# Attention block on one Trainium2 core: the inverse row sums reach the other partitions by VectorE's 32x32 turns and an HBM scratch instead of TensorE transposes

## The reference

```python
def _qkv_attention(qkv):
    bs, length, width = qkv.shape
    ch = width // (3 * N_HEADS)
    q, k, v = jnp.split(qkv, 3, axis=-1)
    scale = 1.0 / np.sqrt(np.sqrt(ch))
    q = (q * scale).reshape(bs * N_HEADS, length, ch)
    k = (k * scale).reshape(bs * N_HEADS, length, ch)
    v = v.reshape(bs * N_HEADS, length, ch)
    weight = jnp.einsum('btc,bsc->bts', q, k)
    weight = jax.nn.softmax(weight.astype(jnp.float32), axis=-1).astype(qkv.dtype)
    a = jnp.einsum('bts,bsc->btc', weight, v)
    return a.reshape(bs, length, -1)

xf = x.reshape(b, -1, c)                      # b = 16, 1024 tokens, c = 512
h = _group_norm(xf, norm_scale, norm_bias)    # 32 groups
qkv = h @ qkv_w + qkv_b
h = _qkv_attention(qkv)                       # 8 heads of 64
h = h @ proj_w + proj_b
return (xf + h).reshape(b, *spatial, c)
```

## Time and profile before

| | us |
|---|---|
| median of 3 runs | 3426.82 (3425.06 to 3427.06) |
| the profiled execution | 3426.32 |
| its span | 3424.6 |
| PE busy in it | 3355.7 (98%) |
| DVE busy | 2813.5 (82%) |
| ACT busy | 2085.2 (61%) |
| POOL busy | 1645.7 (48%) |

### The profile page before, as it was taken

One profiled execution on the slowest core, in us unless ns is written; L12 is line 12 of the kernel. 1 busy time (PEld: TensorE's weight loads), 2 busy tenths in 40 slices (PEclk: granted clock), 3 DMA queues, 4 the chain that ended last, 5 costly groups with the idle time before them and its releaser, 6 DMA issues.

```text
span 3424.6 us, 67790 instructions
## 1 busy us (share of the span) xinstructions
PE 3355.7 (98%) x24640; PEld 2542.3 (74%) x24640; DVE 2813.5 (82%) x3473; ACT 2085.2 (61%) x3985; POOL 1645.7 (48%) x2762
## 2 busy tenths in 40 slices
PE   5999999999999999999999999999999999999998
PEld 4777777777777777777777777777777777777775
DVE  4888888888888888888888888888888888888886
ACT  4666665665665656656666566666566666665663
POOL 3444454545545444544444445445454544454552
PEclk9999999999999999999999999999999999999999
DMA  3878778777887877878788787877878778787777
GB/s 114 194 182 196 193 189 197 183 197 189 192 194 185 197 189 192 197 185 195 187 196 194 186 197 182 198 191 190 196 184 198 191 189 198 182 196 189 185 188 177
DMA packets 255707, 646.87 MB, mean 189 GB/s; under 512 B 73872, under 2 KB 73872, under 8 KB 255376
## 3 DMA queue, kind: packets, MB, share of 16 engines
q1 hardware_dynamic: 235792, 604.79, 74.6%
q10 hardware_dynamic: 19584, 37.76, 3.1%
HBM read 71.84 MB, written 33.55 MB: 31 GB/s over the span
## 4 chain that ended last, share of the span: by engine, by line
PE 88%; DVE 4%; ACT 4%; issue 1%; SPq 1%; POOL 1%; DMA 0%; DVEq 0%; POOLq 0%; ACTq 0%
PE pv_ps L373 23%; PE s_ps L344 22%; PE c_ps L407 7%; PE c_ps L408 7%; PE c_ps L409 7%; PE c_ps L419 3%; PE c_ps L421 3%; PE c_ps L420 3%; PE c_ps L391 3%; PE c_ps L393 3%; PE c_ps L392 3%; PE pv_ps L355 3%; DVE turned L610 2%; ACT staged L495 2%; ACT probs L475 2%; PE s_ps L440 2%
## 5 line engine op out<-in xcount | busy, mean ns | idle before, releaser
L475 ACT ACTIVATE probs<-s_ps,neg_max 128x1024 f32<-128x1024 f32 x1024 | 1140.9, 1115 | 821.6 <-DVE neg_max L627 818.4
L627 DVE TENSOR_REDUCE neg_max<-s_ps 128x1 f32<-128x1024 f32 x1024 | 1205.3, 1219 | 411.4 <-PE s_ps L344 411.4
L610 DVE STREAM_TRANSPOSE turned<-probs 128x1024 f32<-128x1024 f32 x1024 | 1233.6, 1229 | 89.9 <-ACT probs L475 70.4
L373 PE MATMUL pv_ps<-probs_t,v 128*64 128x256 f32 x8192 | 943.7, 383 | 6.7 <-DMA probs_t<-turned 6.7
L373 PEld LDWEIGHTS pv_ps<-probs_t,v 128*64 128x64 f32 x8192 | 567.4, 137 | 358.4 <-issue 99.7
L407 PE MATMUL c_ps<-h_hi,w_hi 128*128 128x256 f32 x2048 | 602.7, 294 | 16.7 <-ACT staged L490 8.9
L408 PE MATMUL c_ps<-h_lo,w_hi 128*128 128x256 f32 x2048 | 580.1, 283 | 0.0
L409 PE MATMUL c_ps<-h_hi,w_lo 128*128 128x256 f32 x2048 | 579.5, 283 | 0.0
L495 ACT ACTIVATE staged<-c_ps,qk_bias 64x256 f32<-64x256 f32 x1024 | 481.0, 470 | 125.8 <-PE c_ps L409 112.4
L783 POOL COPY inv_wide<-inv_sum 128x256 f32<-128x256 f32 x256 | 101.5, 397 | 817.4 <-PE pv_ps L355 810.0
L407 PEld LDWEIGHTS c_ps<-h_hi,w_hi 128*128 128x128 f32 x2048 | 392.8, 192 | 20.7 <-ACT staged L490 10.7
(11 more groups left out here) (71 smaller groups left out, 5094.8 us busy)
## 6 DMA issues: line engine op xcount, KB each, us to landing
probs_t<-turned SPq DMA_DIRECT2D x4096, 128.0 KB, 2.4
x_res<-in_x SPq DMA_DIRECT2D x128, 256.0 KB, 3.0
result<-x_res ACTq DMA_DIRECT2D x128, 256.0 KB, 3.1
x_next<-in_x SPq DMA_DIRECT2D x120, 256.0 KB, 3.5
probs_t<-in_L_conv_qkv_w ACTq DMA_DIRECT2D x4, 768.0 KB, 9.0
turned<-in_x SPq DMA_DIRECT2D x4, 512.0 KB, 13.0
probs_t<-in_L_conv_proj_w ACTq DMA_DIRECT2D x4, 256.0 KB, 14.0
v_bias<-in_L_conv_qkv_b SPq DMA_DIRECT2D x1, 256.0 KB, 17.0
```

The lines of the kernel that those rows point to most:

```text
L373: last = nc.tensor.matmul(pv_ps[side][CH * par:CH * (par + 1), 0, :], v_sb[:, ring_of(i, parity), CH * chunk:CH * (chunk + 1)], p_t[:, par ...
L475: nc.scalar.activation(probs[k % 2][:, :], s_ps[k % 2][:, :], ACT.Exp, bias=neg_max[:, k % 4:k % 4 + 1], accum_out=row_sum[:, (k // HALF) ...
L610: nc.vector.transpose(dst, probs[k % 2][:, :].rearrange("p (k b j) -> p k b j", k=CHUNKS, b=QUADS)).then_inc(probs_turned, 1)
L627: nc.vector.tensor_reduce(neg_max[:, k % 4:k % 4 + 1], s_ps[k % 2][:, :], AX.X, ALU.max, negate=True).then_inc(max_ready, 1)
```

## The change

The inverse takes another way. VectorE writes the four reciprocals of a half into the first 4 columns of a 128x32 tile inv_sum, whose other columns GpSimd sets to 1 once at the start. VectorE turns that tile in 32x32 blocks (turn_inverse, at k = 4n+4, behind the scaling): in each quadrant of 32 partitions the first four now hold the inverses of 32 tokens. ScalarE's queue writes these four rows of each quadrant to an HBM scratch, inv_rows, which then holds four rows of 128 (keep_inverse, four transfers of 4x32, at k = 4n+6), and reads them back at k = 4n+10, each pair of rows repeated over 64 partitions, into inv_wide (spread_inverse, two transfers of 64x2x128). VectorE's scaling now waits for that transfer itself, and multiplies pv_ps by inv_wide. The two transposes on TensorE, GpSimd's copy and ScalarE's copy are gone, and pv_ps needs only half its columns. TensorE's wait for the scaling of two halves ago goes from the transposes to attend.

```diff
 MOVE_LAG = 4
-SPREAD_LAG = 8
+KEEP_LAG = 6
+SPREAD_LAG = 10
 ATTEND_LAG = 10
 EVAC_LAG = 12
...
-        inv_sum = sb("inv_sum", [P, 2, HALF])
-        inv_wide = sb("inv_wide", [P, HALF * CH])
+
+        inv_sum = sb("inv_sum", [P, Q])
+        inv_turned = sb("inv_turned", [P, Q])
+        inv_wide = sb("inv_wide", [P, 2, P])
+        inv_rows = nc.dram_tensor("inv_rows", [2, HALF, P], F32, kind="Internal").ap()
...
-        pv_ps = [ps(f"pv_ps{i}", [P, 2, 2 * P]) for i in range(2)]
+        pv_ps = [ps(f"pv_ps{i}", [P, 2 * P]) for i in range(2)]
...
-            def spread_inverse(b, k):
-                n = (k - SPREAD_LAG) // HALF
-                half, side = 2 * BLOCKS * b + n, n % 2
-                pe.wait_ge(inv_widened, half + 1)
-                at_least(pe, attn_scaled, half - 1)
-                for u in range(2):
-                    last = nc.tensor.transpose(pv_ps[side][:, 1, u * P:(u + 1) * P], inv_wide[:, u * P:(u + 1) * P],
-                                               ident[:, :])
-                last.then_inc(inv_full, 1)
-
             def attend(b, k):
                 n = (k - ATTEND_LAG) // HALF
                 half, side = 2 * BLOCKS * b + n, n % 2
                 i, parity = (n // 2) % 2, (n // 4) % 2
+                at_least(pe, attn_scaled, half - 1)
                 for quad in range(QUADS):
...
-                    if within(s - SPREAD_LAG, N_SLOTS):
-                        spread_inverse(b, k)
...
-            def take_inverse(b, k):
-                n = (k - EVAC_LAG) // HALF
-                half, side = 2 * BLOCKS * b + n, n % 2
-                act.wait_ge(pv_done, half + 1)
-                at_least(act, attn_ready, half)
-                nc.scalar.copy(attn[:, :], pv_ps[side][:, 1, :]).then_inc(inv_taken, 1)
+            def keep_inverse(b, k):
+                n = (k - KEEP_LAG) // HALF
+                half = 2 * BLOCKS * b + n
+                act.wait_ge(inv_turned_ready, half + 1)
+                at_least(act, inv_spread, 32 * (half - 1))
+                for a in range(QUADS):
+                    act.dma_start(inv_rows[n % 2, :, Q * a:Q * (a + 1)], inv_turned[Q * a:Q * a + HALF, :]
+                                  ).then_inc(inv_kept, 16)
+
+            def spread_inverse(b, k):
+                n = (k - SPREAD_LAG) // HALF
+                half = 2 * BLOCKS * b + n
+                act.wait_ge(inv_kept, 64 * (half + 1))
+                at_least(act, attn_scaled, half)
+                for r in range(2):
+                    rows = inv_rows[n % 2, r:HALF:2, :].rearrange("(a u) q -> a u q", a=1)
+                    act.dma_start(inv_wide[CH * r:CH * (r + 1), :, :], rows.broadcast_to([CH, 2, P])
+                                  ).then_inc(inv_spread, 16)
...
-                if k % HALF == EVAC_LAG % HALF and within(s - EVAC_LAG, N_SLOTS):
-                    take_inverse(b, k)
...
+                if k % HALF == KEEP_LAG % HALF and within(s - KEEP_LAG, N_SLOTS):
+                    keep_inverse(b, k)
+                if k % HALF == SPREAD_LAG % HALF and within(s - SPREAD_LAG, N_SLOTS):
+                    spread_inverse(b, k)
                 if k % 16 == 6:
                     store(b, 2 * (k // 16) - 2)
...
-                at_least(dve, inv_widened, half - 1)
-                nc.vector.reciprocal(inv_sum[:, n % 2, :], row_sum[:, n % 2, :]).then_inc(inv_ready, 1)
+                at_least(dve, inv_turned_ready, half)
+                if half == 0:
+                    dve.wait_ge(inv_cleared, 1)
+                nc.vector.reciprocal(inv_sum[:, 0:HALF], row_sum[:, n % 2, :]).then_inc(inv_ready, 1)
+
+            def turn_inverse(b, k):
+                half = 2 * BLOCKS * b + k // HALF - 1
+                dve.wait_ge(inv_ready, half + 1)
+                at_least(dve, inv_kept, 64 * half)
+                nc.vector.transpose(inv_turned[:, :], inv_sum[:, :]).then_inc(inv_turned_ready, 1)
...
-                dve.wait_ge(inv_taken, half + 1)
-                nc.vector.tensor_tensor(attn[:, :], pv_ps[side][:, 0, :], attn[:, :], ALU.mult).then_inc(attn_scaled, 1)
+                dve.wait_ge(pv_done, half + 1)
+                dve.wait_ge(inv_spread, 32 * (half + 1))
+                at_least(dve, attn_ready, half)
+                inv = inv_wide[:, :, :].rearrange("p u q -> p (u q)")
+                nc.vector.tensor_tensor(attn[:, :], pv_ps[side][:, :], inv, ALU.mult).then_inc(attn_scaled, 1)
...
+                if k % HALF == 0 and within(s - HALF, N_SLOTS):
+                    turn_inverse(b, k)
```

More of the change, by code:

```diff
@@ L195, in attention_block @@
         inv_ready = sem("inv_ready")
-        inv_widened = sem("inv_widened")
-        inv_full = sem("inv_full")
-        inv_taken = sem("inv_taken")
+        inv_cleared = sem("inv_cleared")
+        inv_turned_ready = sem("inv_turned_ready")
+        inv_kept = sem("inv_kept")
+        inv_spread = sem("inv_spread")
         pv_done = sem("pv_done")
@@ L373, in attend @@
                         last = nc.tensor.matmul(
-                            pv_ps[side][CH * par:CH * (par + 1), 0, :],
+                            pv_ps[side][CH * par:CH * (par + 1), :],
                             v_sb[:, ring_of(i, parity), CH * chunk:CH * (chunk + 1)],
@@ L712, in _ @@
             nc.gpsimd.memset(group_avg[:, :], 1.0 / GROUP).then_inc(pool_chain, 1)
+            nc.gpsimd.memset(inv_sum[:, :], 1.0).then_inc(inv_cleared, 1)
             nc.gpsimd.memset(half_neg[:, :], -0.5).then_inc(pool_chain, 1)
@@ L773, in split_attn @@
                                         ALU.subtract).then_inc(attn_ready, 1)
-            def widen_inverse(b, k):
-                n = k // HALF
-                half = 2 * BLOCKS * b + n
-                if not within(half, N_HALVES):
-                    return
-                at_least(pool, inv_ready, half + 1)
-                at_least(pool, inv_full, half)
-                sums = inv_sum[:, n % 2, :].rearrange("p (s a) -> p s a", a=1).broadcast_to([P, HALF, CH])
-                nc.gpsimd.tensor_copy(inv_wide[:, :].rearrange("p (s c) -> p s c", s=HALF), sums).then_inc(inv_widened, 1)
             def add_bias(b, n):
@@ L824, in four_slots @@
                     split_qk(b, k, LARGE[m][3][1])
-                widen_inverse(b, k)
                 if k == GROUP_MEAN_SLOT and within(b + 1, BATCHES):
```

## The result

The changed kernel takes 3558.92 us (median of 4 runs, 3556.37 to 3571.1) against 3425.97 us before: a ratio of 1.0395, with an interval of 1.0371 to 1.0419. It is slower by 133 us, where the prediction gave 3396 us in a range of 3380 to 3416. Sign and range were both wrong.

The account below looks back on a forecast made before the run. TensorE's row of work was taken to bound the steady part, SyncE's moves the last 50 us. -37.8 + 5.3 + 2.3 - 0.4 = -30.6 us gave 3396 us, 0.9% faster, range 3380 to 3416.

Parts of the forecast that it names:

- TensorE's saving: Dropping the inverse's two transposes from TensorE's row saves 0.15 us a half, 37.8 us over 252 halves.
- The wait for attn_scaled at attend: TensorE's wait for the scaling of two halves ago, moved from the transposes to attend, costs nothing.
- VectorE's small transpose: New 128x32 transpose on VectorE in each half: 0.15 us, 0.20 with waits, hidden in 35 us free per batch except slot 44.
- Slot 44: Where VectorE's group means release the scores: 0.15 us not gained and 0.20 paid, 15 x 0.35 = +5.3 us.
- The issues on ScalarE: Six DMA issues per half on ScalarE's queue, 0.38 us apart, 2.3 us within 4.06: no exp late, scaling's wait about 0.
- The upper bound of 2.6: VectorE's longest wait for the inverse before scaling: 2.6 us, with issues 0.63 apart and a landing of 4.4.
- The tightest step is that with v: VectorE may be late by about 1.7 us there, 1.5 after the new 0.20; a wait below that costs nothing.
- So this is covered: In the steady part, the store 2.3 us later delays SyncE's residual load and moves, but 7 or 8 us are free.
- The late inverse: Rival, chance 0.12: VectorE scales 2.6 us late in each of 64 steps with v, adding 70 us: 3466.
- The gain taken back elsewhere: Rival, chance 0.16: ScalarE's issues delay exps, or later moves make VectorE wait for turned; 0.1 us a half is 26 us.
- the last case: The rival of the gain taken back elsewhere, 0.16: half at 3408 to 3419, half within 0.2% of before.
- The end: In the last 50 us, the store behind six issues costs +2.3 us; the last half's dropped ScalarE copy gives -0.4.

Follow-up runs that it names:

- e3: The kernel before without the two transposes of the inverse on TensorE, scaling left out of the computation: 3384.47 us, ratio 0.988.
- e5: The changed kernel with the store ahead of the inverse's transfers on ScalarE's queue and the two spreads issued one step earlier: 3389.61 us, 0.9894 of before.
- e1: The changed kernel with the store ahead of the six transfers of the inverse on ScalarE's queue: 3462.12 us, 1.0101 of before.
- e7: The kernel before with 1.3 us of idle VectorE work between scaling and turns, only in steps with k % 16 = 4: 3451.01 us, ratio 1.0073.
- e8: The kernel before with 1.3 us of idle VectorE work between scaling and turns, only in steps with v (k % 16 = 0): 3424.69 us, ratio 0.9997.
- e6: The changed kernel with the spreads one step earlier, the store still behind the four keeping transfers: 3398.77 us, 0.992 of before.
- e2: Two variants of the kernel before: store issued one exp later, 3492.58 us; six unread transfers per half added ahead of the store, 3536.0 us.

## Why the prediction was wrong, point by point

**TensorE's saving: right.** The direct passages gave 0.65 to 0.67 for 0.67 and 0.54 for 0.56, and e3 measured 41 us against 37.8, or 0.16 a half against 0.15.

**The wait for attn_scaled at attend: right.** Between 96 and 3480 us TensorE's list has no wait in attend at all.

**VectorE's small transpose: right in size, and "hidden" only nearly.** It takes 0.201 us in the median of 256, as predicted. Slot 44 went from 8.50 to 8.58 in e5, so +0.08 and not +0.20, and without the transposes it is still 8.49 (e3): the gain of this half was lost as foreseen.

**The issues on ScalarE: mis-sized.** The page of one line's instructions, for the two new lines of the kernel after (ns min/median/max), and the landing of the spreads in us:

```profile
L522 ACTq DMA_DIRECT2D inv_rows<-inv_turned x1024: 245/330/800, 81.9 to 3530.5; - x171
...
L532 ACTq DMA_DIRECT2D inv_wide<-inv_rows x512: 581/620/2167, 95.8 to 3537.3; - x171
...
DMA to landing us min/median/max: 2.6/3.1/5.2
```

The keeps cost 0.33 us each, like the store's 0.34, but the spreads 0.62, which is the price of SyncE's moves. I took one price for both. The last spread went out at 2.1 to 2.4 us instead of 2.0. The median landing of all spreads is the 3.1 that I took, but that of the second one of each pair, for which the scaling waits, is 3.5. So the scaling was 0.4 to 1.1 us late on average by the class of the step (0.56, 1.07, 0.41, 0.81 for k % 16 = 0, 4, 8, 12), where I had put "about 0 in the middle". The upper bound of 2.6 held for these means; the longest single wait is 2.8. The section that the prediction names from the Trainium skill here ("DMA: Bandwidth & Descriptors", Anatomy of one DMA) describes transfers issued from GpSimd, and no run here has one. The store went out at 3.07 instead of 2.3, since the spreads are dearer and there are gaps between the issues; its own issue then takes another 0.61:

```profile
1545.69 1.11 ACT L469 ACTIVATE probs<-s_ps,neg_max 128x1024 f32<-128x1024 f32 x1
1545.76 1.12 ACTq L522 DMA_DIRECT2D inv_rows<-inv_turned  x3
...
1546.90 0.58 ACTq L522 DMA_DIRECT2D inv_rows<-inv_turned  x1
1547.58 1.24 ACTq L532 DMA_DIRECT2D inv_wide<-inv_rows  x2
1548.86 0.61 ACTq L497 DMA_DIRECT2D result<-x_res  x1
```

**"The tightest step is that with v": wrong, and this is one step that failed.** I followed VectorE's delay to the next maximum and its exp (1.5 us free) and not to what stands behind the turns in the same step. In the step with k % 16 = 4 that is the projection's sum, and a bank of TensorE hangs on it with 0.98 us free (0.54 at k = 52). In e5, with the small transpose in and TensorE earlier, 0.81 and 0.37 of that are left, and 1.07 of waiting stand against them. By these rows that loses 0.32 and 0.76 us a time, an estimated 28 us of the 81 that the ledger has at this place; the rest is left to the late moves, which hold up the turn ahead of the sum, and was not taken apart. In e1 the wait in this step is only 0.73 on average, and yet the step is 0.8 to 1.3 us longer than in e5: VectorE comes into it late already. It is ready to scale 3.97 us after the step's first scores in e1, and 3.29 in e5. e7 and e8 show it: the same 1.3 us cost 25 us at one place, 0 at the other.

**"So this is covered": wrong, and this is the dearer one.** I asked of the late store only whether attend would get its moves, with 7 or 8 us free; attend did. But SyncE's queue is in order, and behind the waiting load of the residual stand two other deliveries: the moves that free the buffer turned for VectorE, and the load of x_next for the next batch's transposes. The kernel before has VectorE waiting 0.8 us in all for that buffer. I took that for ample cover; but a wait near zero says only that the buffer was free in time, and not by how much. It was less than the 3 us by which the moves came later.

**The rivals.** The late inverse was given 2.6 us of wait, only at steps with v; it happened with less wait, at another step. The gain taken back elsewhere named the very chain of the store (moves later, VectorE waits for turned), but at a tenth of a microsecond a half. Each was held to cost little or be unlikely by itself; both came in every batch. A price for both at once was missing: e6, e1 and the kernel after stand at +9, +72 and +169 us over e5. The range also left out more than was said: the half of the last case that lies within 0.2% of before (0.08) is outside it too.

**The end.** The +2.3 and -0.4 us at the end can't be told apart from the rest in these runs.

What stays open: the 43 us between the two e2 kernels, and how much of the loss a second buffer for the residual, so that SyncE need not wait for the store, would remove, which no run here has.

## What to carry to other kernels

Before a transfer is put ahead of another on a queue, follow the one that gets later through every waiting instruction behind it, to the last thing in the queue, and not only to the consumer that comes to mind: an engine that waits in order makes a delay of 3 us everyone's. For a delay on an engine that has free time in the mean, look for the smallest reserve behind it, step by step; a mean of 35 us in a batch says nothing of a place where 0.54 us are free. Where a change adds two small delays, price them together too, since both can end at the same place, as here in the steps with k % 16 = 4; and a two-leg trip through HBM is nearly free (5 us here for 256 halves) once the second leg is issued a step earlier and both stand behind, not ahead of, what others wait for.

## What the runs showed of the hardware

An issue on ScalarE's queue has a price by the form of its transfer: 0.33 us for 4x32, 0.62 for 64x2x128 read from HBM with each row repeated. The store behind them takes 0.608 us in the median of the kernel after against 0.339 before; in e5, where it goes first, 0.368. ScalarE's own exps go on beside these issues (the exp at 1545.69 covers the first ones). SyncE's moves did not get longer to issue, though ScalarE's queue was issuing too: 0.59 us in the median of 4096, before and after. They did take longer to land: 2.4 us in the median before, 2.7 after, and 3.0 in e5, which is the fastest of the three all the same; here the order of the issues decided, not the landing of a move.

TensorE's granted clock fell to half for 3.4 us in some places right after one long wait of TensorE: twelve times in the kernel after (waits of 1.9 to 3.4 us), and never between 96 and 3300 us in the kernel before, e3, e5, e6, e7 and e8, where no wait of TensorE there was longer than 1.7 us.
